# Butterfly factors with features on partitions: what it does to a two-layer gated cross-attention kernel

## The reference, cut to what matters

```python
for stage in range(9):                       # s = 1, 2, 4, ..., 256
    s = 2 ** stage; nb = 512 // (2 * s)
    yr = y.reshape(*lead, nb, 2, s)          # partners are s apart
    a, b = yr[..., 0, :], yr[..., 1, :]
    w = weights[stage].reshape(nb, s, 2, 2)
    y = stack([w[..., 0, 0] * a + w[..., 0, 1] * b,
               w[..., 1, 0] * a + w[..., 1, 1] * b])
hidden = gelu(butterfly(x @ W_exp + b_exp, up_weights) + up_bias)
x = x + tanh(g) * (butterfly(hidden, down_weights) @ W_con + b_con + down_bias)
```

## Time and profile before

| | |
|---|---|
| median of 3 runs | 867.05 us (864.64 to 868.33) |
| the profiled execution's time | 869.41 us |
| its span, first to last instruction | 867.7 us |
| mean granted TensorE clock | 0.886 of 2.4 GHz |
| TensorE busy | 730.6 us (84%) |
| VectorE busy | 644.6 us (74%) |
| ScalarE busy | 452.2 us (52%) |
| GpSimd busy | 476.5 us (55%) |

### The profile page before, as it was taken

One profiled execution on the slowest core, in us unless ns is written; L12 is line 12 of the kernel. 1 busy time (PEld: TensorE's weight loads), 2 busy tenths in 40 slices (PEclk: granted clock), 3 DMA queues, 4 the chain that ended last, 5 costly groups with the idle time before them and its releaser, 6 DMA issues.

```text
span 867.7 us, 17744 instructions
## 1 busy us (share of the span) xinstructions
PE 730.6 (84%) x4389; PEld 581.5 (67%) x4389; DVE 644.6 (74%) x3739; ACT 452.2 (52%) x1203; POOL 476.5 (55%) x664
## 2 busy tenths in 40 slices
PE   5734659799999999999999999999999967665596
PEld 4523337667877777787777777787776855554596
DVE  5279992358888888889888888888887788995232
ACT  2212125575767768576666757576765554221131
POOL 2866934346565656565565556565565343663244
PEclk9857569999999999999999999999998885555699
DMA  7900009990000000000000000000000000010672
GB/s 217 423 29 0 1 2 308 309 294 10 2 2 2 2 0 0 0 0 0 0 0 0 0 0 0 0 0 0 0 0 1 2 1 1 25 44 7 178 231 86
DMA packets 36352, 47.20 MB, mean 54 GB/s; under 512 B 2928, under 2 KB 31428, under 8 KB 35921
## 3 DMA queue, kind: packets, MB, share of 16 engines
q1 hardware_dynamic: 31489, 37.45, 14.3%
q10 hardware_dynamic: 3312, 6.03, 2.3%
q0 software_dynamic: 1504, 3.17, 1.0%
HBM read 25.64 MB, written 21.45 MB: 54 GB/s over the span
## 4 chain that ended last, share of the span: by engine, by line
PE 45%; DVE 30%; issue 8%; ACT 6%; DMA 4%; POOL 3%; SPq 3%; DVEq 0%; another core or an unknown queue 0%; POOLq 0%; ACTq 0%
DVE raw L1367 8%; PE bank L747 8%; PE bank L635 7%; DVE raw L1298 6%; DVE m L1361 6%; PE bank L764 4%; PE bank L774 4%; PE bank L765 3%; PE bank L816 3%; DVE negmax L1309 3%; PE bank L735 3%; DMA dn_bias<-in_L_ffn_down_bias 3%; ACT prob L1060 3%; PE bank L833 3%; PE bank L1032 3%
## 5 line engine op out<-in xcount | busy, mean ns | idle before, releaser
L1367 DVE MATCH_REPLACE8 raw<-m,raw 128x77 f32<-128x77 f32 x1024 | 220.1, 222 | 0.0
L1060 ACT ACTIVATE prob<-bank,negmax 128x205 f32<-128x205 f32 x256 | 108.1, 428 | 191.8 <-DVE negmax L1309 191.5
L1361 DVE MAX8 m<-raw 128x8 f32<-128x77 f32 x1024 | 189.2, 226 | 1.1 <-DVE raw L1367 0.3
L487 POOL TENSOR_TENSOR raw<-raw,m 128x616 f32<-128x616 f32 x64 | 77.8, 1216 | 148.6 <-DVEq L1343 148.6
L468 POOL TENSOR_TENSOR prob<-prob,inv 128x820 f32<-128x820 f32 x64 | 101.7, 1589 | 100.1 <-DVE inv L1314 100.1
L747 PE MATMUL bank<-kvT,g_sb 128*128 128x205 f32 x512 | 127.8, 374 | 0.0
L1309 DVE TENSOR_REDUCE negmax<-bank 128x2 f32<-128x410 f32 x128 | 73.9, 577 | 48.7 <-PE bank L747 47.5
L764 PE MATMUL bank<-ptc,kv_ctx 77*128 77x512 f32 x128 | 73.1, 654 | 32.3 <-ACT g_sb L1060 19.8
L747 PEld LDWEIGHTS bank<-kvT,g_sb 128*128 128x128 f32 x512 | 86.0, 196 | 10.7
L833 PEld LDWEIGHTS bank<-v,p1T 77*128 77x128 f32 x512 | 75.0, 217 | 15.3 <-issue 4.4
L833 PE MATMUL bank<-v,p1T 77*128 (+1 forms) x512 | 72.5, 269 | 8.1 <-ACT p1T L1060 3.7
(11 more groups left out here) (207 smaller groups left out, 1380.4 us busy)
## 6 DMA issues: line engine op xcount, KB each, us to landing
z_sorted<-no_row SPq DMA_DIRECT2D x1, 17415.0 KB, 64.2
bf_w<-in_L_ffn_W ACTq DMA_DIRECT2D x23, 256.0 KB, 3.6
bf_w<-in_L_ffn_down_weights SPq DMA_DIRECT2D x1, 4608.0 KB, 14.9
bf_w<-in_L_ffn_up_weights SPq DMA_DIRECT2D x1, 4608.0 KB, 25.5
bf_w<-z_sorted SPq DMA_DIRECT2D x23, 129.0 KB, 3.2
bf_w<-in_L_ffn_W SPq DMA_DIRECT2D x8, 256.0 KB, 4.6
raw<-in_L_xattn_Wkv SPq DMA_DIRECT2D x1, 1024.0 KB, 5.6
cx<-in_ctx SPq DMA_DIRECT2D x1, 616.0 KB
```

The lines of the kernel that those rows point to most:

```text
L1060: return nc.scalar.activation(dst, src, f, **kw)
L1361: v.max(m8[:, h, r, :], sw[:, h, src, :]).then_inc(s[name], 1)
L1367: v.match_replace(sw[:, h, 1, :], m8[:, h, r, :], sw[:, h, src, :], TAKEN)\
```

## The change

The features are put on partitions. The up weights are now `wu` [128, 2, 4, 129]: partition k of chunk c holds feature 128c + k, the 128 inputs lie along the free dimension, and the bias is column 129. The down weights `wd` [128, 2, 4, 128] are `W_con` as loaded. A new value is `own * v + cross * partner`.

- Stages with a distance of 1 to 64 (the "near" ones, `PST` = 7) have their partner on another partition. TensorE exchanges partners by a product with a permutation matrix (`perm`, seven, made by GpSimd at the start) into bank `X`, and a small one into `M` for the bias. GpSimd multiplies by the own coefficients at the same time (`up_part`, `down_part`), and VectorE adds `X` times the cross coefficient, one instruction per chunk.
- Stages 7 and 8 (the "far" ones) have their partner in another chunk of the same partition; VectorE reads it from SBUF.
- Coefficients are loaded once, as columns, by 18 DMAs of 256 runs of 16 B each in place of the two broadcasts; a new job `J_BF` with 14 small products brings them to 128 partitions, and VectorE sorts them with 8 small instructions.
- `J_WCON` goes, `J_WEXP` (transposing `W_exp`) comes. It waits for the semaphore of `W_exp`, `b_exp` and `up_bias`, the last two of which are issued behind the 18. `bias_to_columns` and `down_weight_back` go, `up_weight_back` comes.
- Places: up stages in slots (1,0) to (1,7) and (2,0) as before; down stages 8 and 7 in (0,5) and (0,6), 6 in (1,7), 5 to 0 in (2,0) to (2,5). GpSimd's part stands at the start of the slot, TensorE's at its end, VectorE's at the start of the next.
- `w2`, `z_tile`, `hT`, `rows_out` and others get memory of their own; `y_tile` and `w1_tile` lie in `a_w` and `b_w`. SP waits for the down stages alone before it loads `w2`.

```diff
+        UP_AT = {(1 + n // 8, n % 8): n for n in range(NST)}
+        DOWN_AT = {(0, 5): 8, (0, 6): 7}
+        DOWN_AT.update({(1 + n // 8, n % 8): PST - 1 - (n - 7) for n in range(7, 7 + PST)})
 # SP
-            sp.dma_start(wcon_in[:, :, :], t["L0_ffn_W_con"].rearrange("(c p) d -> p c d", p=128)).then_inc(s["ld_wcon"], 16)
+            sp.dma_start(w_exp[:, :], t["L0_ffn_W_exp"]).then_inc(s["ld_wexp"], 16)
+            for a, name in enumerate(("L0_ffn_up_weights", "L0_ffn_down_weights")):
+                for st in range(PST):
+                    sp.dma_start(bf_k[:, a, st, :, :], t[name][st].rearrange("(c k) a b -> k c (a b)", c=HC))\
+                        .then_inc(s["ld_bf"], 16)
+                for st in range(PST, NST):
+                    sp.dma_start(bf_far[:, a, st - PST, :, :], t[name][st].rearrange("(g p) a b -> p g (a b)", g=2))\
+                        .then_inc(s["ld_bf"], 16)
+            sp.dma_start(wd[:, 0, :, :], ...W_con...)          # then b_exp, up_bias, bq, bk, bv, bo
-            for dst, name, done in ((down_w, ...), (up_w, ...)):
-                sp.dma_start(dst, flat.to_broadcast([128, NBF])).then_inc(s[done], 16)
 # GpSimd
+            for st in range(PST):                                # 21 copies: perm and spread, before the wait on st_c
+                ...
+            def up_part(st):
+                if st == 0: ...wait J_WEXP, ld_wexp, ld_bf, c_coef
+                else: pool.wait_ge(s["up_done"], st)
+                g.tensor_tensor(t_, w, own, ALU.mult).then_inc(s["up_part"], 1)
 # TensorE
+            pe.wait_ge(s["ld_bf"], 16 * 2 * NST)
+            pe.wait_ge(s["c_perm"], 3 * PST)
+            dst = open_job(J_BF)
+            for a in range(2):
+                for st in range(PST):
+                    last = mm(dst[:, at:at + HC * 4], spread[:, st, :], bf_k[...], start=True, stop=True)
+            def up_perm(st):
+                free("M")
+                pe.wait_ge(s["up_done"], st)
+                mm(X[:, :]..., perm[:, st, :], wu[:, 0, :, 0:D], start=True, stop=True).then_inc(s["up_perm"], 1)
+                mm(M[:, 0:HC], perm[:, st, :], wu[:, 0, :, D], start=True, stop=True).then_inc(s["upb_perm"], 1)
+            def down_perm(st):
+                pe.wait_ge(s["up_done"], PST)
+                pe.wait_ge(s["dn_done"], NST - 1 - st)
+                mm(X[:, :]..., perm[:, st, :], wd[:, 0, :, :], start=True, stop=True).then_inc(s["dn_perm"], 1)
 # VectorE
-            def up_stage(cur, part, n, mul, done, rows):   # 2 multiplications and an addition of 512
+            def up_stage(st):
+                dve.wait_ge(s["up_part"], st + 1)
+                if st < PST:
+                    dve.wait_ge(s["up_perm"], st + 1)
+                    for c in range(HC):
+                        v.scalar_tensor_tensor(wu[:, 0, c, 0:D], X[:, 128 * c:128 * c + 128], bf_cross[:, 0, st, c:c + 1],
+                                               wu_t[:, c, 0:D], ALU.mult, ALU.add)
+                    dve.wait_ge(s["upb_perm"], st + 1)
+                    v.tensor_tensor(wub_t[:, :], M[:, 0:HC], bf_cross[:, 0, st, :], ALU.mult).then_inc(s["upb_mul"], 1)
+                    dve.wait_ge(s["upb_mul"], st + 1)
+                    v.tensor_tensor(wu[:, 0, :, D], wub_t[:, :], wu_t[:, :, D], ALU.add).then_inc(s["up_done"], 1)
+                else: ...4 x scalar_tensor_tensor(dst[:, c, :], src[:, far, :], k, wu_t[:, c, :])
+            def down_stage(st):
+                ...the same without the bias, on wd
```

More of the change, by code:

```diff
@@ L16 @@
 AX_X = mybir.AxisListType.X
+AX_XY = mybir.AxisListType.XY
 EPS = 1e-5
@@ L256, in flamingo_kernel @@
         J_CT = J_L1W + 1
-        J_WCON = J_CT + 3
-        J_BO = J_WCON + 1
-        J_K1 = J_BO + 1
+        J_WEXP = J_CT + 3
+        J_BO = J_WEXP + 1
+        J_BF = J_BO + 1
+        J_K1 = J_BF + 1
         J_V1 = J_K1 + 3
@@ L307, in move_jobs @@
                     last = added(bo[:, :], src[:, 0:D])
+                elif k == J_BF:
+                    last = copy(bf_e[:, :, :, :, :].rearrange("p a s c e -> p (a s c e)"), src[:, 0:2 * PST * HC * 4])
                 elif k < J_V1:
@@ L521, in down_stage @@
-                pool.wait_ge(s["dn_mul"], 2 * n + 2)
-                g.tensor_tensor(w_dnT[:, :], dn_t[:, 0, :], dn_t[:, 1, :], ALU.add).then_inc(s["dn_done"], 1)
+                own = bf_own[:, 1, st, :].unsqueeze(2).to_broadcast([128, HC, D]) if st < PST else None
+                w, t_ = wd[:, 1 if n == 1 else 0, :, :], wd_t[:, :, :]
+                if st >= PST:
+                    own = far_own(1, st).unsqueeze(3).to_broadcast([128, 2, 2, D])
+                    w, t_ = (x.rearrange("p (a b) d -> p a b d", a=2) for x in (w, t_))
+                elif n == 2:
+                    pool.wait_ge(s["c_coef"], 8)
@@ L524, in sort_constants @@
+                g.tensor_tensor(t_, w, own, ALU.mult).then_inc(s["dn_part"], 1)
             def sort_constants():
@@ L609, in step @@
                             normalise(A, 3)
-                    for n in DOWN_AT.get((i, slot), ()):
-                        down_stage(n)
                     for b in PLACE_AT.get((i, slot), ()):
@@ L1007, in step @@
                             second_scores(B, 3)
-                        if i == 2:
-                            down_weight_back()
+                    if (i, slot) in UP_AT and UP_AT[i, slot] < PST:
+                        up_perm(UP_AT[i, slot])
+                    if (i, slot) in DOWN_AT and DOWN_AT[i, slot] < PST:
+                        down_perm(DOWN_AT[i, slot])
+                    if (i, slot) == (2, 2):
+                        up_weight_back()
                 now["step"] += 1
@@ L1259, in _ @@
             FIRST = 9
+            dve.wait_ge(s["c_ident"], 1)
+            for st in range(PST):
+                v.tensor_reduce(odd[:, st:st + 1], ident[:, :].rearrange("p (m o w) -> p m o w", o=2, w=2 ** st)[:, :, 1, :],
+                                AX_XY, ALU.add).then_inc(s["c_odd"], 1)
+            dve.wait_ge(s["c_odd"], PST)
+            v.tensor_scalar(even[:, :], odd[:, :], 1.0, -1.0, ALU.subtract, ALU.mult).then_inc(s["c_odd"], 1)
             my_jobs(range(1, FIRST, 2))
@@ new lines, in down_stage @@
+            def down_stage(st):
+                n = NST - 1 - st
+                dve.wait_ge(s["dn_part"], n + 1)
+                if st < PST:
+                    dve.wait_ge(s["dn_perm"], n - 1)
+                    for c in range(HC):
+                        last = v.scalar_tensor_tensor(wd[:, 0, c, :], X[:, 128 * c:128 * c + 128], bf_cross[:, 1, st, c:c + 1],
+                                                      wd_t[:, c, :], ALU.mult, ALU.add)
+                else:
+                    src, dst = (wd[:, k, :, :] for k in ((0, 1) if n == 0 else (1, 0)))
+                    if n:
+                        dve.wait_ge(s["dn_done"], n)
+                    for c in range(HC):
+                        k, far = far_cross(1, st, c)
+                        last = v.scalar_tensor_tensor(dst[:, c, :], src[:, far, :], k, wd_t[:, c, :], ALU.mult, ALU.add)
+                last.then_inc(s["dn_done"], 1)
@@ L1446, in step @@
                         close_top()
+                    before = slot_before(i, slot) if i is not None else None
+                    if before in UP_AT:
+                        up_stage(UP_AT[before])
+                    if before in DOWN_AT:
+                        down_stage(DOWN_AT[before])
+                    if (i, slot) == (2, 2):
+                        dve.wait_ge(s["up_done"], NST)
+                        v.tensor_tensor(bias_cols[:, :], wu[:, 0, :, D], up_bias[:, :], ALU.add).then_inc(s["biases_ready"], 1)
                     if (i, slot) in ((17, 1), (20, 2)):
```

239 lines of the change are left out of this document (133 added, 106 removed).

## The result

The changed kernel took 886.05 us (885.12 to 890.66, 4 runs) beside 867.69 us (864.64 to 869.32, 4 runs) of the kernel before on the same chip: a ratio of 1.0226, with a 95% interval of 1.0181 to 1.0272. The forecast was 831 us, range 816 to 853: faster, where the kernel became slower.

A forecast was written before the change was run, and what follows sets the result against it. VectorE was taken to bind step 1 and TensorE everything from step 2 on. The terms 2 - 36 - 2.4 = -36.4 us took the profiled 869.4 to 833.0 us, median 831 us, range 816 to 853.

The forecast's parts named there:

- Step 3 and all behind it keep their work: Step 3 and everything after it, loop included: work unchanged by the change, costed at nothing.
- a shift of step 3's start moves the end by as much: From step 3 (start 163.18 us) on: an earlier start ends the kernel equally earlier, as long as TensorE stays the bound.
- if step 3 and those behind it become longer than before: Sign that the prediction is wrong: step 3 or later steps lengthen; step 3 was expected at 35 us again.
- The signs that were named for the part up to step 3: VectorE below 20 us in step 1, clock above 0.8, first maxima at 48 to 60, some 38 later, and 125 to 130.
- The start of step 1: Set-up up to step 1's first maxima: from 49.05 to about 51 us, +2 us, range -1 to +11.
- the 14 products: `J_BF` in the set-up: 14 products of 16 columns at 0.2 us, 2.8 us, upper end 3.4 us.
- VectorE's chain behind the last jobs: Set-up, from the last jobs' end at 42.5 us to step 1's first maxima at 50.8 us: 8.3 us.
- Step 1: Step 1, 73.8 us before: VectorE no longer binds, TensorE's work plus waits take 38 us, -36; ends 33 and 55.
- The instructions with both inputs in SBUF: `wu` sums and far stages on VectorE: waiting out GpSimd was taken as 0, at most 11 x 1.55 us.
- Step 2: Step 2, 40.4 us before: TensorE's work plus waits and some lower clock take 38 us, -2.4, range 34 to 46.
- (a): Rival, steps 1 and 2: hand-overs bind without overlap, 97 us for 16 slots instead of 76; median 852 us; chance 0.12.
- (d): Rival, set-up: small loads alone make it slower, above 146 ns a run; at 200 ns median 886 us; chance 0.03.

The follow-up runs named there:

- e1: The changed kernel with 62 idle semaphore increments on VectorE ahead of its set-up jobs: 833.23 us, ratio 0.9631 to the kernel before.
- e6: The changed kernel with 121 idle semaphore increments on VectorE ahead of its set-up jobs: 887.73 us (one run).
- e9: The kernel before with 20 idle semaphore increments ahead of VectorE's loop: 867.48 us, ratio 0.9995.
- e2: The changed kernel with 128 idle semaphore increments on VectorE ahead of its set-up jobs: 888.05 us, ratio 1.0248 to the kernel before.
- e3: The kernel before, without the change, with 66 idle semaphore increments on VectorE ahead of its set-up jobs: 922.35 us, ratio 1.0634.
- e8: Changed kernel, 16 increments, loads reordered, down coefficients on ScalarE's queue, and `J_BF` behind the layer-1 jobs: 821.98 us, ratio 0.9458 to the kernel before.
- e7: Changed kernel, 16 increments, biases and small loads issued ahead of coefficients, down coefficients on ScalarE's queue: 829.57 us, ratio 0.9547 to the kernel before.
- e11: Changed kernel with 58 increments, VectorE's near stages on one chunk of four; compared with the changed kernel with 16 increments: 835.76 us.
- e10: Changed kernel with 16 increments, its 14 permutation products 8 columns wide; compared with the changed kernel with 16 increments alone: 833.91 us.

## Why the prediction was wrong, by its steps

**The step that failed** is the one that had a cost of nothing: "Step 3 and all behind it keep their work", with the sentence ahead of it that a shift of step 3's start moves the end by as much. VectorE's work was kept, to the instruction. Its time was not: 51.5 us went in the loop. VectorE stood for 39.2 us in its two gaps at nine jumps back; TensorE, which binds there, was 23.2 us longer idle and 28.3 us longer busy at a lower clock. The prediction counted what the change adds to each engine's time, and never what it adds to an engine's program ahead of the loop. It even named the sign ("if step 3 and those behind it become longer than before") but gave it no chance, and no rival had the mechanism. That the place of VectorE's loop decides is shown by e1 to e6, and by e9 as the control. That the places repeat after 128 instructions rests on one shift by 128 (e2) and on the size of the packets. That the reason is a fetch at each jump back is argued from the packets and the gaps, which come and go with the loss. That four blocks in place of three are what it takes is an inference: a body of 271 instructions that begins in the last 14 places of a block is also one that ends in the first 14 of another, and no run had a body of another length. Why it costs five packets a pass, why the gap falls in two pieces at one place and in one at another, and where the blocks begin, stays open.

The Trainium skill (Runtime: NRT & Kernel Launch, "Instruction fetch mechanics") says that most engines hold 512 instructions, filled in blocks of 256, and that a taken branch to a block that isn't held forces a fetch before the engine goes on. The trace agrees with the second part, with 2.95 and 1.58 us of "issue" behind the jump. It does not agree with the size: a packet of queue 14 is 8 KB, 128 instructions, and a shift by 128 (e2) left the kernel as slow as it was, while one by 62 (e1) took 53 us off. By blocks of 256 a shift of 128 would have put the body elsewhere in its block.

**The rest of the forecast, read at a good place.** e1 differs from the changed kernel only in the place of the loop, and its profiled execution took 832.6 us where the sum said 833.0; its median 833.2 where 831 was said. The first of these is closer than the forecast was good: that execution was the fastest of its four, and the sum started from 869.4 us, more than any of the four runs of the kernel before beside the result. By the medians 32.7 us were won (865.93 to 833.23) where 36 were forecast. Like for like the change is worth a ratio of 0.963, at good places (e1 to before) and at bad ones too (888.05 / 922.35, e2 to e3). Two of the terms missed in opposite ways as well, so the agreement is partly luck. The signs that were named for the part up to step 3 all came: VectorE busy for less than 20 us in step 1, first maxima at 56.6, 91.6 and 129.35 us, a clock of 0.96. The terms:

- *The start of step 1*, forecast 51 (+2 us), came at 56.6 (+7.5 us), inside its range of -1 to +11. Several sizes were off. An issue of a coefficient load took 0.56 to 0.90 us, not 0.43; the timeline of SP:

```profile
16.60 4.67 SPq L365 DMA_DIRECT2D bf_k<-in_L_ffn_up_weights  x7
21.31 1.80 SPq L368 DMA_DIRECT2D bf_far<-in_L_ffn_up_weights  x2
23.16 4.55 SPq L365 DMA_DIRECT2D bf_k<-in_L_ffn_down_weights  x7
27.75 1.12 SPq L368 DMA_DIRECT2D bf_far<-in_L_ffn_down_weights  x2
```

  The job that was held up was not `J_BO` but the transposition of `W_exp`, which I had costed at nothing: it waits for both bias rows, which stand behind the coefficients. `J_BO` itself came at 35.18 us, 3 us behind the 32.1 that I had for it. And the 14 products took 6.15 us, not 2.8, at half clock behind a gap of 8.8 us (in e8, where TensorE comes to them busy, 3.50 at 0.92). The forecast had misread its row: a product of this type stands in the profile as two records, so 14 products are the x28 below, and 0.24 us in the earlier trace rows is half a product. TensorE's timeline:

```profile
33.14 1.12 PE L677 MATMUL bank<-ident,w_exp 128*128 128x128 f32 x4 [8.82 <-DMA up_bias<-in_L_ffn_up_bias]
35.18 0.76 PE L736 MATMUL bank<-l_wT,bv 128*128 128x128 f32 x2 [0.92 <-ACT wu L1130]
35.87 6.15 PE L744 MATMUL bank<-bf_k,spread 64*128 64x16 f32 x28
```

  VectorE's chain behind the last jobs was 6.0 us (50.6 to 56.6) where I had 8.3. The 16-byte runs themselves were cheaper than both of my values, 17 and 38 ns. From 22 to 30 us hardly anything else moved:

```profile
q1 hardware_dynamic: 3264, 0.05, 21.9%
```

  That is an estimate of 0.219 x 8 x 16 / 3264 = 8.6 ns a run; the engines were idle for most of the time, and a load landed some 2 to 3 us after its issue. The queue was held up by issuing, not by moving. e8 shows what was to be had: 13.1 us, by the order of the loads, a second queue for half of the coefficients and the later place of `J_BF` together (the first two alone, e7: 4.9).
- *Step 1*: 38 forecast, 35.0 measured. The multiplications are gone, and the near stages cost what the earlier trace rows gave: 351 ns forecast, 343 measured. The instructions with both inputs in SBUF, for whose meeting GpSimd I took 0, paid something: three of the seven `wu` sums took 0.17 us, the others 0.59 to 0.82. Of the far stages' 16 instructions the median is 0.35 us, but one of `wu` took 1.68 and one of `wd` 1.12. That is some 4 us together, of the 17 that the range allowed, and by e11 less work on VectorE would have shortened step 1 by nothing:

```profile
L1383 DVE SCALAR_TENSOR_TENSOR wu<-bank,bf_cross,wu_t 128x128 f32<-128x128 f32 x28 | 7.8, 343 | 2.9 <-PE bank L921 2.9
...
L1388 DVE TENSOR_TENSOR wu<-wub_t,wu_t 128x4 f32<-128x4 f32 x7 | 3.1, 442 | 0.2
```

  TensorE's waits in steps 1 and 2 were 4.4 us together, where I counted 6.
- *Step 2*: 38 forecast, 37.8 measured. The clearing of `z_sorted`, issued earlier, cost nothing: step 3 took 35.10 us where the earlier trace rows have 35.08.
- *Rivals.* The hand-overs in their full price (a) wanted 97 us for steps 1 and 2, which took 72.8. The small loads alone (d) would have made nothing slower: the start lost 7.5 us, and 38.4 would have been needed, with 146 ns a run. The result lay on the side of this last rival, even at its figure of 886 us, by accident: its mechanism was not at work, and none of the rivals had the one that was.

## What to carry to other kernels

A loop in an engine's program has a place, and what stands ahead of it moves the loop: here 66 instructions more on VectorE cost 5.4 us and more a pass, over all more than the change had won, and 7, 16 or 62 idle increments gave it back. When code far from an edit becomes slower, compare the packets of the instruction queues of the two profiles, and look for "issue" at the jump back before looking for contention; and compare two versions of a kernel with their loops at good places, or the difference is that of the places. When loads are put in a queue, put last those that the first jobs don't need, and let the jobs that need them stand last too: here this and a second queue were worth 13 us.

## What was not expected of the hardware

- VectorE's loop at a bad place: 5 instruction packets of 8 KB a pass in place of none, 2.95 + 1.58 us of standstill at the jump, 44.2 us a pass in place of 38.8. Queue 8, whose 0.33 MB are about the size of TensorE's program, carried the same 20 packets in every run, though TensorE's loop has 554 instructions.
- Work taken from TensorE can leave a step as long as it was: in step 1 of e10 an estimated 26.4 us of work in place of 31.2, a clock of 0.85 in place of 0.99, and 34.3 us in place of 33.8 to 35.8 (one profiled execution).
- Loads of 256 runs of 16 bytes cost at the issue: 0.56 to 0.90 us each on the issuing queue, where the loads of weights just ahead of them take 0.43, while the DMA engines were busy for 0.22 of the time.
